# Router logits and their turning as full 128 x 128 matmuls, gate columns kept beside the expert columns, and a new order of steps, in a transformer block on one core

## What is computed

```python
x = L0_attn_x                                    # (8, 512, 256)
mod = (silu(c) @ wmod).reshape(8, 6, 1, 256)     # sa, ca, ga, sb, cb, gb; ga, gb clipped
h = layernorm(x) * (1 + ca) + sa
# attention: 16 heads; content part (16) through latents of 192 and 64, rotary part (64), causal
c_q = h @ w_dq.T;  q = [c_q @ w_uq.T | rope(c_q @ w_qr.T)]
c_kv = h @ w_dkv.T; k = [c_kv @ w_uk.T | rope(h @ w_kr.T)];  v = c_kv @ w_uv.T
x = x + ga * (softmax(q @ k.T * SCALE + causal) @ v) @ w_out.T
h = layernorm(x) * (1 + cb) + sb
logits = h @ gate_weight.T                       # 32 routed experts
top_val, top_idx = top_k(softmax(logits), 8);  top_val /= top_val.sum()
w_tg = weights of the 8 groups (merge_groups[top_idx], one-hot)
act = silu(h @ gate_g.T) * (h @ up_g.T)          # 8 groups, 96 wide each: 768 columns
out = x + gb * sum_g w_tg[:, g] * (act_g @ down_g)
```

## Time and profile before

| | |
|---|---|
| runs of the kernel before | 1019.28, 1019.88, 1020.67 us; median 1019.88 |
| the profiled execution | 1020.3 us, its span 1018.6 us |
| PE busy | 962.8 us |
| DVE, POOL, ACT busy | 685.2, 496.8, 426.2 us |
| granted PE clock, mean | 0.981 |

### The profile page before, as it was taken

One profiled execution on the slowest core, in us unless ns is written; L12 is line 12 of the kernel. 1 busy time (PEld: TensorE's weight loads), 2 busy tenths in 40 slices (PEclk: granted clock), 3 DMA queues, 4 the chain that ended last, 5 costly groups with the idle time before them and its releaser, 6 DMA issues.

```text
span 1018.6 us, 23971 instructions
## 1 busy us (share of the span) xinstructions
PE 962.8 (95%) x9847; PEld 704.9 (69%) x9847; DVE 685.2 (67%) x1371; ACT 426.2 (42%) x780; POOL 496.8 (49%) x462
## 2 busy tenths in 40 slices
PE   5789999999999999999999999999999999998897
PEld 3546667766687677866777667866778667875566
DVE  5676767675776757667676758777576766766334
ACT  5234444264433634344442644245443445333332
POOL 2345454673545552663625644555526636356202
PEclk9889999999999999999999999999999999999999
DMA  6322010210102101200102101030002101011000
GB/s 205 81 87 84 33 62 2 75 63 2 63 1 95 43 11 53 73 33 33 63 2 73 64 2 63 7 99 33 33 33 73 49 17 63 1 53 64 2 1 21
DMA packets 37599, 48.73 MB, mean 48 GB/s; under 512 B 9386, under 2 KB 23210, under 8 KB 37490
## 3 DMA queue, kind: packets, MB, share of 16 engines
q1 hardware_dynamic: 37490, 47.20, 13.9%
HBM read 17.80 MB, written 4.21 MB: 22 GB/s over the span
## 4 chain that ended last, share of the span: by engine, by line
PE 75%; DVE 9%; ACT 6%; POOL 4%; issue 3%; DMA 2%; SPq 2%; POOLq 0%; DVEq 0%; ACTq 0%
PE ring L1206 15%; PE ring L1053 11%; PE ring L1054 9%; PE ring L1055 9%; PE ring L1178 7%; PE av L1222 7%; ACT pt L746 3%; DVE mcol L943 3%; PE ring L1283 2%; PE ring L1285 2%; PE ring L1284 2%; DVE prod L919 2%; PE ring L1190 2%; PE ring L1114 1%; SPq L537 1%
## 5 line engine op out<-in xcount | busy, mean ns | idle before, releaser
L746 ACT ACTIVATE pt<-ring 128x384 f32<-128x384 f32 (+1 forms) x384 | 171.0, 533 | 256.7 <-PE ring L1206 226.8
L943 DVE TENSOR_REDUCE mcol<-ring 128x1 f32<-128x128 f32 (+3 forms) x512 | 211.1, 482 | 47.8 <-PE ring L1183 47.2
L624 POOL TENSOR_SCALAR_AFFINE_SELECT pt<-pt 128x512 f32<-128x512 f32 x128 | 81.0, 646 | 215.4 <-ACT pt L746 215.4
L919 DVE TENSOR_TENSOR prod<-ring,table 128x1024 f32<-128x1024 f32 x128 | 154.5, 1217 | 44.4 <-PE ring L1055 40.1
L1206 PE MATMUL ring<-rows 32*128 32x512 f32 (+3 forms) x3072 | 172.2, 329 | 6.5 <-ACT pt L746 5.3
L1206 PEld LDWEIGHTS ring<-rows 32*128 32x128 f32 x3072 | 127.4, 184 | 53.4 <-issue 20.4
L597 POOL TENSOR_TENSOR rows<-prod,rows 128x1024 fp32r<-128x1024 f32 x64 | 152.6, 2390 | 17.3 <-ACT rows L725 16.4
L590 POOL TENSOR_TENSOR prod<-prod 128x512 f32<-128x512 f32 x64 | 82.0, 1281 | 87.2 <-DVE prod L919 86.6
L1178 PE MATMUL ring<-rows 32*128 32x512 f32 (+3 forms) x1024 | 89.9, 361 | 16.3 <-DMA cont<-h_lo 4.7
L725 ACT ACTIVATE rows<-prod 128x1024 fp32r<-128x1024 f32 x64 | 67.7, 1073 | 88.0 <-POOL prod L591 83.1
L1222 PE MATMUL av<-pt,vals 128*17 128x512 f32 (+3 forms) x1024 | 87.3, 447 | 4.3 <-POOL pt L624 4.3
(11 more groups left out here) (189 smaller groups left out, 1798.5 us busy)
## 6 DMA issues: line engine op xcount, KB each, us to landing
cont<-h_hi SPq DMA_DIRECT2D x96, 128.0 KB, 2.0
cont<-h_lo SPq DMA_DIRECT2D x96, 128.0 KB, 2.0
xn<-x_dram SPq DMA_DIRECT2D x8, 512.0 KB, 4.7
xr<-x_dram SPq DMA_DIRECT2D x8, 512.0 KB, 4.2
out_dram<-xr SPq DMA_DIRECT2D x8, 512.0 KB, 3.2
...
```

Of the source, the lines that this page charges most:

```text
L746: sc.activation(pt[:, PT_AT[n] + h * w:PT_AT[n] + (h + 1) * w], ps[:, 0:w], ACT.Exp, scale=SCALE).then_inc(exp_ready.sem, 1)
L919: ve.tensor_tensor(prod[:, s % PROD, :, :], ps[:, :].unsqueeze(1).broadcast_to([P, 2, S]), table[:, :, :], ALU.mult).then_inc(rotated.sem, 1)
L943: last = ve.reduce_max(mcol[:, q, h * HR + ONE_ROW:h * HR + ONE_ROW + 1], ps[:, at:at + (q + 1) * P], AX_X)
```

## The change

Four edits. The gate columns (32) and the gate and up columns (1536) come to lie in one tile, gwu, in this order; gw and gu are views of it. logits uses the first 128 columns, so the gate columns and the first 96 of the others, and its result has 128 rows, of which 32 are wanted; in batch 0 it waits for the split of the gate and up columns. lgT has all 128 partitions, and logits_copy copies them. turn_l multiplies lgT, 128 rows and 128 columns of it as the stationary side, by the first 32 columns of the identity, so four fp32 matmuls stand in the place of four transposes. BODY_ORDER and LAST_ORDER list the same steps in a new order; SETUP_ORDER stays.

```diff
-rope.0200 score.000 rotate.0200 load_next.1 rope.0201 exp.000 loads.0 maxima.010 rotate.0201 clear.000 qcon.01
+maxima.010 rope.0200 reduce.010 load_next.1 score.000 rotate.0200 rope.0201 exp.000 score.001 rotate.0201 stats1.1
...
-        gu_hi, gu_lo = sb("gu_hi", [P, EC, 2 * G * FI], F32R), sb("gu_lo", [P, EC, 2 * G * FI], F32R)
-        gw_hi, gw_lo = sb("gw_hi", [P, EC, NX], F32R), sb("gw_lo", [P, EC, NX], F32R)
+        gwu_hi, gwu_lo = (sb(n, [P, EC, NX + 2 * G * FI], F32R) for n in ("gwu_hi", "gwu_lo"))
+        gw_hi, gw_lo, gu_hi, gu_lo = (w[:, :, cols] for cols in (slice(0, NX), slice(NX, NX + 2 * G * FI)) for w in (gwu_hi, gwu_lo))
...
-        lgT = room[0:NX, 2, :]
+        lgT = room[:, 2, :]
...
-                        sc.activation(lgT, ps[0:NX, :], ACT.Copy).then_inc(logits_copied.sem, 1)
+                        sc.activation(lgT, ps[:, :], ACT.Copy).then_inc(logits_copied.sem, 1)
...
                     elif kind == "logits":
                         ps = take_bank(pe, b, part, step)
-                        three(ps[0:NX, :], *columns(gw_hi, gw_lo, 0, NX), *rows2,
+                        if isinstance(b, int) and b == 0:
+                            pe.wait_ge(ffn_split, EC)
+                        three(ps[:, :], *columns(gwu_hi, gwu_lo, 0, P), *rows2,
                               ready=lambda c: wait(pe, lo_ready[1], b, ahead, c)).then_inc(full_sem, 1)
...
                         for t in range(TT):
-                            last = pe.transpose(av[:, t * NX:(t + 1) * NX], lgT[:, t * P:(t + 1) * P], ident[0:NX, 0:NX])
+                            last = pe.matmul(av[:, t * NX:(t + 1) * NX], lgT[:, t * P:(t + 1) * P], ident[:, 0:NX], start=True, stop=True)
```

More of the change, by code:

```diff
@@ L89 @@
-pow1.1 value.010 exp.011 maxima.020 combine.030 norm1.1 rope.0311 reduce.020 score.012 clear.011 rotate.0311
-maxima.021 combine.031 exp.012 move_q.03 maxima.022 hi.030 move_k.03 reduce.021 hi.031 clear.012 turn1.10 reduce.022
-turn1.11 lo.030 modulate1.10 value.011 modulate1.11 low1.10 shift.02 maxima.030 shifted.02 low1.11 value.012
-reduce.030 score.020 attn_out.01 score.021 exp.020 maxima.031 clear.020 exp.021 value.020 reduce.031 clear.021 lo.031
-maxima.032 value.021 reduce.032 score.022 shift.03 exp.022 rope.1000 shifted.03 clear.022 score.030 rotate.1000
@@ L104 @@
-gated.05 inner_lo.02 weighed.03 weigh.05 weighed.04 inner_hi.03 maxima.102 upped.05 inner_lo.03 down.00 weighed.05
-inner_hi.04 reduce.102 inner_hi.05 inner_lo.04 inner_lo.05 lo.110 shift.10 join.00 down.01 combine.111 shifted.10
-hi.111 join.01 lo.111 store.0
+maxima.010 rope.0200 reduce.010 load_next.1 score.000 rotate.0200 rope.0201 exp.000 score.001 rotate.0201 stats1.1
+combine.020 rope.0210 exp.001 maxima.011 rotate.0210 clear.000 rope.0211 reduce.011 pow1.1 maxima.012 rotate.0211
+clear.001 value.000 reduce.012 combine.021 value.001 score.002 shift.01 exp.002 kcon.01 shifted.01 qcon.01 clear.002
@@ new lines @@
+score.010 qcon_hi.01 kcon_hi.01 qcon_lo.01 hi.020 kcon_lo.01 move_q.02 value.002 lo.020 rope.0300 move_k.02 exp.010
+score.011 rotate.0300 hi.021 clear.010 attn_out.00 lo.021 rope.0301 exp.011 maxima.020 rotate.0301 clear.011 value.010
+reduce.020 combine.030 maxima.021 rope.0310 reduce.021 score.012 rotate.0310 rope.0311 exp.012 move_k.03 maxima.022
+norm1.1 loads.0 move_q.03 rotate.0311 clear.012 value.011 reduce.022 combine.031 value.012 hi.030 turn1.10 turn1.11
+modulate1.10 shift.02 lo.030 shifted.02 modulate1.11 low1.10 score.020 hi.031 low1.11 attn_out.01 maxima.030 exp.020
@@ new lines @@
+move_k.10 rope.1100 move_q.11 mixed.01 hi.101 rope.1101 move_k.11 stats2.0 rotate.1100 pow2.0 values.10 maxima.100
+rotate.1101 values_out.10 norm2.0 maxima.101 reduce.100 combine.110 turn2.00 turn2.01 reduce.101 modulate2.00
+rope.1110 lo.101 modulate2.01 rope.1111 low2.00 low2.01 maxima.102 rotate.1110 logits.0 rotate.1111 gate.00 reduce.102
+combine.111 logits_copy.0 turn_l.0 tanh.00 gate.01 gated.00 top.0 gate.02 ex.0 tanh.01 top2.0 up.00 tanh.02 gate.03
+upped.00 gated.01 turn_w.0 up.01 wT.0 hi.110 wT_lo.0 gate.04 gated.02 tanh.03 gated.03 weigh.00 upped.01 tanh.04
@@ new lines @@
+maxima.010 qcon.01 reduce.010 score.000 qcon_hi.01 qcon_lo.01 rope.0200 exp.000 score.001 rotate.0200 clear.000
+value.000 exp.001 maxima.011 clear.001 rope.0201 reduce.011 maxima.012 rotate.0201 rope.0210 reduce.012 combine.020
+kcon.01 rope.0211 kcon_hi.01 rotate.0210 score.002 rotate.0211 kcon_lo.01 combine.021 shift.01 exp.002 move_q.02
+value.001 shifted.01 score.010 hi.020 move_k.02 clear.002 hi.021 lo.020 value.002 exp.010 attn_out.00 maxima.020
+rope.0300 reduce.020 clear.010 lo.021 score.011 rotate.0300 value.010 exp.011 maxima.021 clear.011 rope.0301
@@ new lines @@
+reduce.021 score.012 rotate.0301 value.011 exp.012 move_q.03 maxima.022 move_k.03 rope.0310 clear.012 reduce.022
+combine.030 loads.0 rope.0311 rotate.0310 shift.02 value.012 shifted.02 hi.030 rotate.0311 score.020 attn_out.01
+combine.031 score.021 exp.020 hi.031 clear.020 lo.030 exp.021 maxima.030 value.020 reduce.030 lo.031 maxima.031
+maxima.032 reduce.031 clear.021 value.021 reduce.032 score.022 shift.03 exp.022 shifted.03 score.030 clear.022
+value.022 score.031 exp.030 attn_out.02 clear.030 exp.031 wofold.0 value.030 score.032 clear.031 value.031 exp.032
@@ L111 @@
+upped.03 inner_hi.02 weigh.03 upped.04 weigh.04 inner_lo.02 up.05 weighed.03 weighed.04 inner_hi.03 weigh.05 upped.05
+down.00 inner_lo.03 weighed.05 inner_hi.04 inner_lo.04 inner_hi.05 inner_lo.05 down.01 join.00 join.01 store.0
 """
```

29 lines of the change are left out of this document (14 added, 15 removed).

## The result

The changed kernel is slower: a median of 1028.97 us (7 runs, 1025.11 to 1032.40) beside 1019.88 us (7 runs of before), a ratio of 1.009 with a 95% interval from 1.0067 to 1.0113. The forecast was 1020.4 us, hardly to be told from no change, in a range from 1011 to 1027; the median lies above it. The profiled execution of the changed kernel is one of its short ones, 1025.5 us with a span of 1023.8; so of the 9.1 us between the medians the two traces show 5.2, 3.5 lie between this execution and the median of its kernel, and the other 0.4 between the profiled execution of before and its median.

What follows compares the result with a forecast made beforehand. TensorE, busy 95% of the span, was taken as the bound. Middle batches +0.6, batch 0 +2.0 and last batch -2.1 sum to +0.5 us on 1019.88: 1020.4 us, 8-in-10 range about 1011 to 1027.

Steps and rivals of the forecast that it cites:

- The front: Middle batch, score.012, maxima.021 and maxima.022: set apart by other steps, both maxima lose their bank waits, -1.3 us a batch.
- The row of four groups: Middle batch, score.020, maxima.030, score.021, maxima.031 in succession, four banks each: bank waits cost +0.3 us (0 to 1.3).
- the hold: Middle batch, PE idle ahead of score.020, which needs VectorE's shifted.02 right after shift.02: +0.9 us (0 to 1.6).
- lo.110: Batch's end, POOL does it between inner_lo.02 and inner_lo.03, delaying down.00: mostly hidden, +0.4 us a batch (0 to 2.4).
- The last batch: value.011's wait -0.5, turning +0.3, tail -1.9 as earlier selection lets down.00 run through: sum -2.1 us.
- The start of batch 0: stats1.1 waits for xn's load on VectorE, holding rotations, reductions and PE's banks: +2.0 us (0 to 3.5).
- rival 3: stats1.1 waits for its load in every batch, VectorE and PE's banks 1 us later: 1027.4 us, chance 0.12.
- rival 2: Clock falls in every middle batch, at turn1's and shift.02's transposes plus a hold: 1024.0 us, chance 0.18.
- rival 1: Clock no longer falls in four batches, as the waits in the maxima groups go: 1015.6 us, chance 0.28.
- the turning: Logits turned by four fp32 matmuls (eight passes) instead of four transposes on PE: +0.33 us a batch (0 to +1.2).
- the logits: Six matmuls with 128 instead of 32 stationary columns: at most 0.4 us gained in all, taken as 0.
- shift.02 without idle: Middle batch, a second value step ahead of shift.02 covers most of its 0.70 us idle: -0.55 us.

Runs made afterwards that it cites:

- groups_in_row: Kernel before with maxima.030 moved from ahead of score.020 to behind it in batches 0 to 6: 1031.3 us, ratio 1.0103.
- lo_late: Changed kernel with lo.110 behind inner_lo.05 on POOL, as before, in batches 0 to 6: 1026.3 us, ratio 1.0071.
- the second: Trace of the changed kernel run once more, unaltered, to see a longer execution: 1029.6 us, profiled at 1031.5.
- old_last: Changed kernel with LAST_ORDER of before: 1028.2 us, ratio 1.0089.
- edits_alone: Changed kernel with BODY_ORDER and LAST_ORDER of before, so only the wide logits and new turning: 1023.0 us, ratio 1.0029.

## Why the prediction was wrong

Three steps of the sum failed in their mechanism, and one term was missing from it.

- **The front**, -1.3 us a batch, gave -0.8. The step that failed is that both maxima shed their waits once a step stands between them. maxima.022 did (0.97 us for 1.99, more than the 0.6 put on it). maxima.021 did not: 1.72 us for 1.40 in most batches, where -0.7 was forecast, since its fourth bank still waits for VectorE to read maxima.020; and score.012, not in the sum, became 0.4 longer. Over seven batches that is 3.5 us. The bound "VectorE must still read every bank" was what happened to one of the two.
- **The row of four groups** was put at +0.3 us, "since the hold just ahead of them leaves time for banks to come free". It measured +0.7 in the changed kernel and as much in groups_in_row without a hold, 2.5 us over seven batches more than forecast. The banks are not held by old readers, which a hold could help: apart from three of maxima.030's, the row waits for banks that it fills itself, for the exponentials and the reductions of its own groups.
- **lo.110** was put at +0.4 us in every batch. It is nothing in six batches and 3.9 us in batch 0, 2.9 of them back in down.00 of lo_late: 1.1 us more than forecast, in one place. I had looked at POOL's queue in the last batch, not in the first, where the split of the down weights stands ahead of it.
- **The last batch**: -2.1 forecast, -0.5 measured in the traces, nothing in the medians. The tail did what was said: from turn_l to the end of down.00 the batch is 1.5 us shorter with the new turning in it (-1.9 + 0.3 forecast). The front gained nothing: it is 2.7 us ahead of before at score.020 and level with it again at shift.03, behind the groups in between. What failed is a term that isn't in the sum: the unread matmuls moved behind mix left it at half clock, 1.5 us, less 0.5 that turn2 and the logits gained behind it. The row at 967.21 was there to say what mix costs.
- **The start of batch 0** came near for another reason, so by luck. +2.0 on top of the front's -1.3 makes +0.7; the end of maxima.022 was 0.5 us later in the first trace and 2.1 in the second, 1.2 of these lost ahead of the batch. But stats1.1 did not wait for xn in any batch of the trace, which also puts rival 3 out: the hold at score.000 did it.
- **The clock**: rival 2 had more falls at 1.2 us each, at the transposes, and 1024.0 us. No trace of the changed kernel has a fall at turn1: twelve transposes with 0.89 us of idle behind them ran at 1.00 (351.69 to 354.38). The rule of the Trainium skill, TensorE: Matmul & The Clock Gate, Part 4, that transposes don't count as busy in the same way, pointed at the wrong place here: the longer row of transposes had no fall. The falls came some 8 us behind the start of turn1, in score.021, mostly at 2.7 us each (one of the four at 1.1); none in the trace of old_last, with the same order of batches 0 to 6, one in the first trace and three in the second. In exchange the four at turn1 went, some 5 us together. So by its falls the first trace is 2 to 3 us better off than before, and the second 1 to 2 us worse off: they spread the executions and are not the main loss. That the old falls would go with the waits ahead of them was the thought of rival 1; it isn't shown, as groups_in_row has these waits too and no fall at turn1.
- **The range.** Halfway to the bounds of each piece, added up for seven batches, the sum runs from -6.5 to +21 us, not from -3 to +4. With its own bounds the forecast would have held the result.
- **Right** were the turning (+0.35 for +0.33), the logits at no cost, the hold (0.89 for 0.9) and shift.02 without idle (-0.7 for -0.55). The Trainium skill's rule on changes of the tiling mode (TensorEngine Tiling (Array Packing), Key Properties) would, by the estimate above, have taken 1.6 us off; edits_alone, 3.6 us slower with turnings worth 2.8, shows no such gain for 32 stationary columns.

Added up, the front, the row, lo.110 and the last batch (3.5, 2.5, 1.1 and 1.6 us, less 1.0 at shift.02) are 7.7 of the 8.6 us between the forecast and the median. These are differences of single traces; the medians of the runs agree in kind (the turning 2.9 us, lo.110 2.7, the unread matmuls 2.7), but spread by some 5 us each.
